# Moving the value products to the end of TensorE's slot in a batched attention block, with one wait for both heads

## What is computed

```python
h = jnp.maximum(_layernorm(x, axis=-1), 0.0)
q, k, v = (split_heads(h @ W.T) for W in (Wq, Wk, Wv))
a = jnp.einsum('bhnd,bhmd->bhnm', q, k) * D ** (-0.5) + (adj + adj)[:, None]
a = jnp.where(jnp.any(a != 0, axis=-1, keepdims=True), a, -jnp.inf)
p = softmax(a, axis=-1)            # rows that are all NaN become 0
o = jnp.einsum('bhnm,bhmd->bhnd', p, v)
out = x + o.transpose(0, 2, 1, 3).reshape(B, N, D) @ Wo.T
```

## Time and profile before

| | us |
|---|---|
| median of 3 runs | 1287.07 |
| lowest, highest | 1287.06, 1287.58 |
| the profiled execution | 1287.33 |
| its span, first to last instruction | 1285.5 |
| busy in the span: PE, DVE, ACT, POOL | 1245.4, 1114.6, 1054.7, 884.3 |

### The profile page before, as it was taken

One profiled execution on the slowest core, in us unless ns is written; L12 is line 12 of the kernel. 1 busy time (PEld: TensorE's weight loads), 2 busy tenths in 40 slices (PEclk: granted clock), 3 DMA queues, 4 the chain that ended last, 5 costly groups with the idle time before them and its releaser, 6 DMA issues. The chain is left out here.

```text
span 1285.5 us, 43965 instructions
## 1 busy us (share of the span) xinstructions
PE 1245.4 (97%) x13104; PEld 1109.5 (86%) x13104; DVE 1114.6 (87%) x4006; ACT 1054.7 (82%) x2427; POOL 884.3 (69%) x1262
## 2 busy tenths in 40 slices
PE   4899999999999999999999999999999999999996
PEld 4788988888988888988888988888988888888885
DVE  6798889888889898889898889898889898888884
ACT  4788888888888888888888888888888888888885
POOL 1676677776677776777776777776777766777765
PEclk9999999999999999999999999999999999999999
DMA  6344554554544554554554544554544554544541
GB/s 228 84 108 119 143 122 118 143 131 116 145 122 116 145 130 114 147 122 115 147 129 114 149 121 114 148 127 114 151 119 114 150 125 115 152 118 114 135 116 57
DMA packets 90772, 163.88 MB, mean 127 GB/s; under 512 B 14976, under 2 KB 23168, under 8 KB 90752
## 3 DMA queue, kind: packets, MB, share of 16 engines
q1 hardware_dynamic: 90752, 163.64, 48.9%
HBM read 46.14 MB, written 16.78 MB: 49 GB/s over the span
## 5 line engine op out<-in xcount | busy, mean ns | idle before, releaser
L884 POOL TENSOR_TENSOR fold<-minus 128x512 f32<-128x512 f32 x256 | 327.4, 1279 | 293.6 <-DVE bounds L739 293.5
L567 ACT ACTIVATE probs<-minus,bounds 128x256 f32<-128x256 f32 x1024 | 459.5, 498 | 23.8 <-DVE bounds L739 23.8
L748 DVE TENSOR_TENSOR pT_lo<-pT_ps,pT_hi 128x512 f16<-128x512 f32 x512 | 351.3, 686 | 62.5 <-ACT pT_hi L578 59.3
L578 ACT ACTIVATE pT_hi<-pT_ps 128x512 f16<-128x512 f32 x512 | 304.9, 595 | 109.7 <-PE pT_ps L403 108.1
L739 DVE CUSTOM_DVE_ANT_0 minus<-s_ps,adj_now 128x256 f32<-128x256 f32 x1024 | 388.5, 416 | 5.9 <-ACT probs L567 4.7
L403 PE MATMUL pT_ps<-ident,probs 128*128 128x128 f32 x2048 | 307.6, 273 | 1.8 <-ACT probs L567 1.6
L328 PE MATMUL job_ps<-hT_hi,w_hi 128*128 128x256 f16 x1024 | 280.2, 274 | 1.4 <-DVE w_lo L689 0.9
L328 PE MATMUL job_ps<-hT_hi,w_lo 128*128 128x256 f16 x1024 | 279.0, 272 | 0.0
L328 PE MATMUL job_ps<-hT_lo,w_hi 128*128 128x256 f16 x1024 | 278.8, 272 | 0.0
L403 PEld LDWEIGHTS pT_ps<-ident,probs 128*128 128x128 f32 x2048 | 241.8, 140 | 19.4 <-ACT probs L567 3.0
L392 PE MATMUL s_ps<-qk_stack 96*128 96x256 f32 x1024 | 246.4, 323 | 0.7 <-DVE w_lo L689 0.7
(11 more groups left out here) (77 smaller groups left out, 2253.0 us busy)
## 6 DMA issues: line engine op xcount, KB each, us to landing
qk_stack<-qk_parts SPq DMA_DIRECT2D x768, 128.0 KB, 2.3
x_in<-x SPq DMA_DIRECT2D x32, 512.0 KB, 3.4
x_res<-x SPq DMA_DIRECT2D x32, 512.0 KB, 3.7
out<-y SPq DMA_DIRECT2D x64, 256.0 KB, 2.1
adj_in<-adj SPq DMA_DIRECT2D x32, 256.0 KB, 3.5
w_in<-wq SPq DMA_DIRECT2D x2, 512.0 KB, 6.7
w_in<-wk SPq DMA_DIRECT2D x2, 512.0 KB, 8.2
w_in<-wv SPq DMA_DIRECT2D x2, 512.0 KB, 7.9
```

Source lines behind the costliest of these rows:

```text
L567: end = nc.scalar.activation(probs[hh % 2][:, t, :], minus[hh // 2 % 2][:, hh % 2, t, :], ACT.Exp, bias=bounds[:, hh // 2 % 4, 2 * (hh % 2 ...
L578: nc.scalar.activation(pT_hi[hh % 4][:, :, :], pT_ps[hh % 2][:, :].rearrange("p (m n) -> p m n", m=NT), ACT.Copy).then_inc(pT_high, 1)
L748: nc.vector.tensor_tensor(pT_lo[hh % 4][:, :, :], pT_ps[hh % 2][:, :].rearrange("p (m n) -> p m n", m=NT), pT_hi[hh % 4][:, :, :], ALU.sub ...
L884: nc.gpsimd.tensor_tensor(f1[:, :, :], src[:, :, 0:N // 2], src[:, :, N // 2:N], ALU.add).then_inc(folded1, 1)
```

## The change

In PE's `body` the loop over the slot's jobs now stands ahead of the value products of even slots, so that these come last in the slot. In `values` the wait for `pT_split` is made once, ahead of the first head of the pair, for both heads. No instruction is added to or removed from PE, ACT, DVE or POOL but for one register instruction on PE in such a slot, and the other engines' lists are as they were.

```diff
@@ -413,7 +413,9 @@
                     pe.wait_ge(factor_ready, b * PAIRS + hh // 2)
 
-                pe.wait_ge(pT_split, head_no(b, hh) + 1)
+                if hh % 2 == 0:
+
+                    pe.wait_ge(pT_split, head_no(b, hh) + 2)
                 for t in range(NT):
@@ -470,13 +472,14 @@
                     elif not last:
                         scores(b + 1, hh + AHEAD - HEADS)
 
+                    for kind, n, d, start, stop in jobs_at(hh, first, last):
+                        job(kind, n, d, start, stop, b)
+
                     for was in range(hh - 2, hh) if hh % 2 == 0 else ():
                         if was >= 0:
                             values(b, was, first and was < 2)
                         elif not first:
                             values(b - 1, HEADS + was, False)
-                    for kind, n, d, start, stop in jobs_at(hh, first, last):
-                        job(kind, n, d, start, stop, b)
```

## The result

The changed kernel takes 1427.51 us (median of 4 runs, 1424.16 to 1428.97) against 1287.3 us for the kernel before: a ratio of 1.1085, 95% interval 1.1065 to 1.1106. The profiled execution took 1428.29 us with a span of 1426.5. The forecast was 1436, slower, in a range of 1398 to 1468.

The account below looks back on a forecast made before the run. PE's own list of work was taken as the bound (busy 97%). Five terms sum to 4.83 us a batch; 31 x 4.83 - 0.7 = 149 us on 1287.33 gives 1436, range 1398 to 1468 (chance 0.86).

Parts of the forecast that it names:

- slot 14, "v" 0 behind "y" 1: ACT's take of "y" 1 ends later, at 616.85, so "v" 0 starts at 616.92 instead of 616.26: +0.66 us a batch.
- slot 2, "v" 3 behind "qk" 3: Late pT_hi and pT_lo delay DVE's take of "qk" 3, for which "v" 3 waits: +1.3 us a batch, gain of 0.37 included.
- slots 3 and 4: DVE's take of "o" 1 comes late behind pT_lo, and "y" 0 in slot 4 waits for it: +1.16 us a batch.
- slot 5, "h" 1 behind "h" 0: ACT takes "h" 0 only after late copy and exponentials, so "h" 1 starts at T5 + 2.78, not 1.37: +1.41 us.
- slot 6, "qk" 0 behind "y" 0 and both "h": "qk" 0 waits for the take of "h" 1 and starts at T6 + 0.89; value products follow: +0.3 us a batch.
- the other ten slots: Slots such as 0, 8, 10 and 12 find their banks free, and slots 7 to 12 cost nothing: 0 us.
- What bounds the kernel now: PE's list of work is the time: busy 97% of the span, 39.80 of 40 us mid-loop, where it does not wait.
- What goes: Slot 2's value products no longer wait for head 1's low part: 0.37 us a batch, 11 to 12 us, at least 7.5.
- faster, 1275.6: Rival: all banks are free in time, only the gain of 0.37 us a batch remains, 1275.6 us; chance 0.03.
- The mechanism: ACT's copy L556, heading odd slots, starts 0.27 us after their transposes and delays what follows; jobs want banks 0.46 us sooner.
- Cover alone: Rival: ACT and DVE take banks at today's times, only the value products' place costs: 1.14 us a batch, 1322; chance 0.05.
- clock rival: PE's five pauses also halve its clock once a batch, adding up to 3.4 us: 255 us in all, 1541; chance 0.05.

Follow-up runs that it names:

- e11: Kernel before, with DVE's statistics of the next input moved from slot 0 to three parts in slots 7, 9 and 11 of the batch before: 1265.62 us, ratio 0.9831.
- e1: Kernel before, with only the joint wait for both heads' low parts, value products still ahead of the jobs: 1288.49 us, ratio 1.0010.
- e8: Kernel before, with DVE's statistics of the next input moved from slot 0 to slot 9 of the batch before, in one piece: 1280.95 us, ratio 0.9952.
- e4: Value products behind the jobs in slot 4 only, compared with the kernel before: 1342.65 us, ratio 1.0429.
- e5: Value products behind the jobs in slot 14 only, compared with the kernel before: 1309.93 us, ratio 1.0176.
- e3: Value products behind the jobs in slots 8 and 10 only, compared with the kernel before: 1289.55 us, ratio 1.0023.
- e10: Changed kernel, with ACT's takes moved ahead of the copy L556 and exponentials in odd slots, DVE's takes ahead of L757 and L761: 1385.4 us, ratio 1.0764.
- e6: Changed kernel, with ACT's copy L556 moved to the end of its odd slot and DVE's L757, L761, L770 behind takes and pT_lo: 1461.76 us, ratio 1.1359.

## Why the prediction was right, point by point

| term, us a batch | predicted | measured |
|---|---|---|
| slot 14, "v" 0 behind "y" 1 | 0.66 | 0.58 |
| slot 2, "v" 3 behind "qk" 3 | 1.3 | 1.13 |
| slots 3 and 4 | 1.16 | 1.11 |
| slot 5, "h" 1 behind "h" 0 | 1.41 | 1.32 |
| slot 6, "qk" 0 behind "y" 0 and both "h" | 0.3 | 0.25 |
| the other ten slots | 0 | 0.10 |
| sum | 4.83 | 4.49 |

**What bounds the kernel now** was read rightly in the main: PE's own list. But that PE does not wait in the middle of the loop, read from 39.80 busy us in 40, was too strong: e11 took 0.74 us of waiting out of each batch, 21 us in all. The busy time hides such waits, since matmul records overlap. In slot 2 of the kernel before, the last product of head 0 and the first of head 1 start 0.38 us apart instead of 0.03, and 0.20 of it shows as idle:

```profile
625.58 0.18 PE L425 MATMUL o_ps<-v_parts,pT_lo 128*128 128x33 f16 x1
625.96 0.20 PE L424 MATMUL o_ps<-v_parts,pT_hi 128*128 128x65 f16 x1 [0.20 <-DVE pT_lo L748]
```

**What goes.** The 0.37 us in slot 2 were in the rows, but a plain gain of that size was never there to be had: in e1 the value products of slot 2 wait longer and the kernel loses almost nothing, because "v" 3 behind them waits for DVE's take anyway. The 7.5 us of the earlier trace rows were therefore no lower bound of a gain. Both waits have one cause, the statistics, and e8 and e11 show that it must be treated there. The rival "faster, 1275.6" would have failed for this reason too.

**The mechanism** held in both parts. e4 shows them side by side, 0.47 of cover in slot 4 and 1.32 of a late take in slot 5, and e5 the long arm of the late copy into slot 2, though by the factor and not by the take of "qk" 3. In slots 3 and 4 "h" 0 waits 0.45 for the take of "v" 3, which the prediction did not have; it falls inside the wait for the take of "o" 1 and does not set the length. e3 bears out that the slots whose banks are free cost nothing but the 0.03 us named below. The copy starts 0.27 us after T15 as forecast, and 0.19 after T5.

**Sizes.** Every term came out 4 to 17% smaller than predicted, for several small reasons that point one way.

- *Slots 2 to 4, ACT's "v" take.* I had put it at 0.36 us, from two rows of which the second, `pT_hi` at 618.66, had waited for the transposes of T15 (618.03 and 0.60 long) and not for ACT. In slot 15 of the changed kernel its step is 0.26 (685.95 to 686.21), and `pT_hi` ends at T15 + 2.20 instead of 2.31. DVE's `pT_lo` then starts 2.24 after T15 instead of 2.38, its chain to the end of the take of "qk" 3 takes 7.81 us where I had 7.82, and "v" 3 starts at T15 + 10.11 instead of 10.27. From T15 to T3 this batch took 10.90 us, 1.22 more than before; the 1.13 in the table is the part of it in slot 2 itself.
- *Slot 5, which has no "v" take.* The copy starts at T5 + 0.19 instead of 0.27, ACT's take of "h" 0 lasts 0.58 and not 0.60, and the two that wait behind it start 0.04 and 0.05 after it instead of 0.07: "h" 1 starts at T5 + 2.63 instead of 2.78.
- *Slot 14.* "v" 0 starts 3.79 after T13 (679.05) where 3.84 was forecast, and 0.04 of the delay is counted in slot 13.

The 0.07 from the end of a take to the instruction that waited for it was 0.04 to 0.06 at most places and 0.13 at "y" 0.

**Rivals.** Cover alone (1322) is out by e4 and e10. The clock rival did not come true in the changed kernel, whose loop ran at 1.00, with waits of up to 1.41 us in the batch shown. It was not far off, as e6 shows below, but its price there was 0.56 us a batch and not the 3.4 allowed for it.

## What to carry to other kernels

A group of products placed between the start of a slot and a job that needs a bank is cover for the emptying of that bank; before it is moved, look up when each following job's bank was emptied, and how long before the job. Then follow whoever waits for the *moved* group: if it stands at the head of an in-order list, everything behind it is late, takes of other banks included, and the loss can appear in a slot in which nothing was changed. When a short wait has a cause upstream, here 1.6 us of statistics in one piece, cut it up and move it to where that engine is idle; moving the waiting side only changes which instruction waits.

## What the runs showed of the hardware

**The clock fell behind a wait of 2 us, in most batches but not in all.** In e6 PE waits longer for the take of "qk" 3 than in the changed kernel (2.02 against 1.41 us). The row of PE with the wait, then the granted clock of the stretch behind it and of the one ahead (third number from the end):

```profile
533.84 0.28 PE L328 MATMUL job_ps<-w_hi,hT_hi 128*128 128x256 f16 x1 [2.02 <-DVE qk_parts L714]
```

```profile
534.30:537.80 3.50, 3.50 (x32) 2.93 (x30) 2.22 (x9) 1.67 (x4) 3.20 (x4) 0.51 0.66 150
520.00:534.30 14.30, 11.71 (x132) 10.37 (x130) 12.38 (x45) 11.06 (x27) 8.68 (x14) 1.00 0.35 102
```

In this batch, from half a microsecond behind the wait, the clock stands at its 1.2 GHz level for some 3.4 us in which PE never pauses. Such a stretch recurs in 23 of the loop's 30 batches, and the mean granted clock over the span is 0.968 against 0.994 for the changed kernel, whose clock stays at 2.4 GHz throughout the loop. The Trainium skill, "TensorE: Matmul & The Clock Gate", section "A second HAM failure mode: psum-queue depth-cycling", describes such swings from waits for PSUM banks; e6 agrees with it, the changed kernel, with five such waits a batch, does not. The wait alone does not decide: in the other seven batches of e6 it stands in the same place, 2.02 us and more, and the clock stays up, as here:

```profile
975.76 0.28 PE L328 MATMUL job_ps<-w_hi,hT_hi 128*128 128x256 f16 x1 [2.02 <-DVE qk_parts L714]
967.10:1010.80 43.70, 38.81 (x411) 34.23 (x410) 34.70 (x125) 31.99 (x76) 27.28 (x40) 1.00 0.44 114
```

What tells the two kinds apart is open. Comparing them gives the clock's price (medians of 23 and of 7 batches): slot 3 takes 3.58 us against 2.14, but slot 4, where PE then waits less, takes 3.67 against 4.68, and the batch 44.28 against 43.72. The slow stretch costs 0.56 us a batch, 13 us of the 174 that e6 lost, because most of it goes into time that PE would have waited away.

**Transposes right behind value products cost some 0.03 us.** Odd slots 7, 9, 11 and 15 are 0.03 to 0.04 us longer in the changed kernel, in e3 slots 9 and 11 alone. Slot 12, whose six wide float32 products no longer follow the value products, is 0.09 shorter. What of the change from one kind of product to the next does this wasn't tested.
